# Hybrid attention and FFN pair on one core: the first row maxima of the plain layer from key differences, fills and masks on GpSimd, and the first causal maxima inside the last chunk turns

## The chip, the cores and the metric

The kernel runs on one core of a Trainium2 chip. The metric is the device time of one execution in microseconds; lower is better. The kernel before takes 1384.7 us (median of 3 runs, 1383.22 to 1387.49).

## The reference, cut to what matters

The input x has 4 sequences of 1024 tokens with 128 channels. Two layers follow each other, each an attention with 16 heads of 8 channels and then a gated FFN of width 384. The first attention is plain, the second causal. All of it is float32.

```python
x = x + attn_a(layernorm(x))      # softmax(q k / sqrt(8)) v, all keys
x = x + ffn(layernorm(x))         # silu(x wg) * (x wu), times wd
x = x + attn_b(layernorm(x))      # the same with keys after the query masked out
x = x + ffn(layernorm(x))
```

The softmax needs, for each head and query, the maximum of the scores over its keys. The change is about how and when the first of these maxima are taken.

## The kernel before, in words

**Windows.** Each layer has 16 windows: one sequence and a group of 4 heads. A window needs q and k of its heads as operands `qop` and `kop`. They are split in a high and a low part (`split_parts`, L746 for the subtraction, ScalarE's rounding copy L570), stored to DRAM and loaded again by SyncE (`store_parts` L343 and L345, `load_operands` L356 and L359, 14 transfers for a window) into one of 3 buffers. Rows of the operand buffers that no transfer fills hold ones (`kop`) or zeros (`qop`). For buffers 1 and 2 GpSimd sets the ones (L466) and ScalarE the zeros (`clear_query_rows`, L534).

**Jobs.** The row maxima come from "jobs". A job is one TensorE matmul (L993) of 128 queries with up to 512 keys into a bank of a ring in PSUM, and one VectorE reduction of that bank into a column of `maxima`: L804 (plain maximum), or L801 (add the causal mask, then maximum; a second instruction reads the accumulator) where the tile crosses the diagonal. In layer 0 a window has 64 jobs of 512 keys, two (kh 0 and 1) for each head and query block, in a ring of 4 banks (3 to 6). In layer 1 a window has 48 jobs of 128 to 512 keys and the ring has 3 banks (4 to 6).

**Shift.** When a half window (32 jobs in layer 0, 16 and 32 in layer 1) is done, VectorE negates and merges the maxima (`negate_max`, L810), GpSimd splits them in two bf16 parts (`split_shift`, L486, L488), TensorE transposes them (L1025), ScalarE copies them to `shift_rows` (L615), and SyncE moves them into rows of `qop` (`shift_to_operand`, two small transfers at L393). Only then can TensorE make the real scores of that half with the maximum subtracted (L1007, masks by L1015), ScalarE take the exponential (L599) and TensorE the weighted sums (L1041).

**Order.** All engines walk one list per layer, `plan.walk`, built from a string of letters: "job", "shift", "scores", "sums", "norm". Jobs run ahead of the scores: layer 0 starts with 48 jobs before its first scores (the shift of the first half stands behind job 37), layer 1 with 44 (its shift stands behind job 35). In these two heads of the walks the maxima run with little beside them. In layer 0 TensorE also transposes the FFN weights there (L969, after jobs 19, 23 and 27) and spreads the second layer's biases (L925 to L927), and GpSimd converts weights and builds the masks (L442 to L461) before the ones of L466. SyncE loads window 1's operands (`load_operands(1, 1)`) before it enters the walk, when both fills and all the stores of the last chunks are done. It works through its list in order, so a shift's transfers queue behind that load.

**Chunk turns.** Between the two attentions `stages` runs turns over 8 chunks of 512 tokens: output projection, residual, FFN, and, in layer 0, the qkv products of layer 1 for the chunk before. Turn 7 has `down(7)` (L1116), the addition to x (L726), the moments (L707, L711), `normalise` (L718) and the qkv products of chunk 6. Turn 8 has those of chunk 7 (L944, L946), with `add_v` (L737) and `split_parts`. Layer 1's walk begins after turn 8, though window 0's operands are loaded long before: by then all of sequence 0 is done.

## Time and profile before

| what | value |
|---|---|
| median of 3 runs | 1384.7 us |
| the profiled execution, its own time | 1387.37 us |
| its span, first to last instruction | 1385.3 us |
| mean granted TensorE clock | 0.967 |
| busy: TensorE, VectorE, ScalarE, GpSimd | 96%, 86%, 73%, 10% |

The sums of the prediction are made against the profiled execution, which is the longest of the runs shown. Busy shares are shares of the span; TensorE's records have modelled ends, so its share says little by itself. Times of instructions in the sections below are microseconds from the start of the span.

### The profile page before, as it was taken

The page shows a single profiled execution, that of the slowest core. Times are in us where ns is not written, and L with a number is a line of the kernel's source. Part 1 is how long each engine was busy: PE and PEld are TensorE (multiplying, and loading weights), DVE is VectorE, ACT ScalarE, POOL GpSimd, SP SyncE. Part 2 cuts the span into 40 slices and gives each one's busy share as a digit, 9 for nine tenths or more (in the row PEclk, how much of TensorE's full clock was granted, in tenths as well). Part 3 has the DMA queues.
Part 4 walks back from the last instruction along what each step waited for, and adds up shares of the span by engine and source line. Part 5 has one row for each costly group of instructions (what it writes and reads, how often), then busy time and mean ns, then how long its engine had stood idle before and what let it go on. Part 6 is the DMA issues. An engine that isn't in the chain of part 4 may idle for free.

```text
span 1385.3 us, 26773 instructions
## 1 busy us (share of the span) xinstructions
PE 1336.7 (96%) x9681; PEld 688.9 (50%) x9681; DVE 1193.6 (86%) x2979; ACT 1005.4 (73%) x1791; POOL 131.9 (10%) x301
## 2 busy tenths in 40 slices
PE   9899999999999999999997988999999999999898
PEld 6444444444444444444435765555555555555477
DVE  7899999999999999999935977788888888888366
ACT  8478888888888888888884542577777776777743
POOL 5320000000000000000001210200000000000011
PEclk9689999999999999999999995799999999999999
DMA  7611011111001111101000433122111211130001
GB/s 210 188 31 32 8 26 32 32 32 32 17 17 32 33 32 32 27 7 32 2 1 1 116 100 90 32 47 50 33 34 39 57 33 33 36 59 5 2 24 39
DMA packets 40059, 58.43 MB, mean 42 GB/s; under 512 B 7796, under 2 KB 19448, under 8 KB 39928
## 3 DMA queue, kind: packets, MB, share of 16 engines
q1 hardware_dynamic: 39928, 56.72, 17.2%
q8 instruction: 77, 1.26, 0.4%
q14 instruction: 54, 0.44, 0.1%
HBM read 36.77 MB, written 18.87 MB: 40 GB/s over the span
## 4 chain that ended last, share of the span: by engine, by line
PE 84%; DVE 7%; ACT 5%; issue 3%; DMA 0%; POOL 0%; DVEq 0%; SPq 0%; ACTq 0%; POOLq 0%
PE psum L1041 28%; PE psum L993 26%; PE psum L1007 16%; ACT probs L599 4%; PE psum L933 4%; PE psum L1116 3%; DVE maxima L804 3%; PE psum L1106 2%; PE psum L1015 2%; PE psum L944 1%; PE psum L1057 1%; DVE hid L870 1%; DVE junk L801 1%; PE psum L918 1%; PE psum L946 1%
## 5 line engine op out<-in xcount | busy, mean ns | idle before, releaser
L599 ACT ACTIVATE probs<-psum 128x512 f32<-128x512 f32 (+3 forms) x1408 | 833.7, 659 | 217.4 <-PE psum L1007 116.2
L804 DVE TENSOR_REDUCE maxima<-psum 128x1 f32<-128x512 f32 x1280 | 801.9, 681 | 29.5 <-PE psum L993 23.4
L993 PE MATMUL psum<-kop,qop 62*128 62x512 f32 (+3 forms) x1792 | 590.1, 448 | 11.0 <-DVE maxima L804 5.2
L1007 PE MATMUL psum<-qop,kop 64*128 64x512 f32 (+3 forms) x1792 | 526.0, 422 | 6.7 <-ACT probs L599 3.0
L993 PEld LDWEIGHTS psum<-kop,qop 62*128 62x128 f32 x1792 | 281.8, 192 | 394.3 <-DVE maxima L804 299.2
L1041 PE MATMUL psum<-probs,v 128*32 128x512 f32 (+3 forms) x3584 | 439.9, 563 | 0.7 <-ACT probs L599 0.7
L1007 PEld LDWEIGHTS psum<-qop,kop 64*128 64x128 f32 x1792 | 268.4, 188 | 76.1 <-ACT probs L599 44.6
L801 DVE CUSTOM_DVE_ANT_0 junk<-psum,mask 128x384 bf16<-128x384 f32 (+3 forms) x512 | 232.2, 485 | 53.5 <-PE psum L993 51.5
L1041 PEld LDWEIGHTS psum<-probs,v 128*32 128x32 f32 x3584 | 70.9, 108 | 100.9 <-issue 67.7
L1015 PE MATMUL psum<-half_ident,key_mask 64*128 64x64 bf16 x1024 | 89.6, 197 | 0.0
L496 POOL TENSOR_TENSOR att<-att_raw,rden 128x128 f32<-128x128 f32 x64 | 26.1, 407 | 512.4 <-DVE rden L815 512.4
L486 POOL TENSOR_TENSOR shift<-negmax,zeros 128x16 bf16<-128x16 f32 x64 | 14.1, 220 | 569.2 <-DVE negmax L810 569.2
L1106 PE MATMUL psum<-ffn_xt,gate_up_w 128*128 128x512 f32 x192 | 53.8, 417 | 5.4 <-DVE hid L870 5.3
L1015 PEld LDWEIGHTS psum<-half_ident,key_mask 64*128 64x128 bf16 x1024 | 49.5, 96 | 17.4 <-issue 7.3
L1116 PE MATMUL psum<-down_w,hid 128*128 128x128 f32 x384 | 46.4, 277 | 6.4 <-DVE hid L870 6.4
L678 ACT ACTIVATE hid<-psum 128x512 f32<-128x512 f32 x48 | 28.6, 597 | 30.7 <-PE psum L1106 30.4
L615 ACT CAST shift_rows<-psum 32x128 f32<-32x128 bf16 x64 | 16.0, 250 | 46.1 <-PE psum L1025 46.1
L1116 PEld LDWEIGHTS psum<-down_w,hid 128*128 128x128 f32 x384 | 44.1, 192 | 8.7 <-DVE hid L870 8.7
L815 DVE RECIPROCAL rden<-att_raw 128x16 f32<-128x16 f32 x64 | 15.6, 243 | 36.9 <-ACT att_raw L620 36.9
L726 DVE TENSOR_TENSOR x<-psum,x 128x512 f32<-128x512 f32 x32 | 22.1, 689 | 28.3 <-PE psum L1116 15.6
L933 PE MATMUL psum<-ident,sums 128*128 128x128 f32 x256 | 41.1, 283 | 5.0 <-ACT sums L606 1.6
L801 DVE DVE_READ_ACCUMULATOR2_ANT maxima<- 128x1 f32 x512 | 42.5, 83 | 0.1
(92 smaller groups left out, 693.7 us busy)
## 6 DMA issues: line engine op xcount, KB each, us to landing
qop<-q_parts SPq DMA_DIRECT2D x256, 64.0 KB
kop<-k_parts SPq DMA_DIRECT2D x64, 128.0 KB
kop<-k_parts SPq DMA_DIRECT2D x128, 64.0 KB
q_parts<-parts SPq DMA_DIRECT2D x24, 256.0 KB, 2.9
k_parts<-parts SPq DMA_DIRECT2D x24, 256.0 KB, 3.2
x<-in_L_attn_a_x SPq DMA_DIRECT2D x8, 256.0 KB, 4.8
q_parts<-att SPq DMA_DIRECT2D x8, 256.0 KB, 3.8
k_parts<-att SPq DMA_DIRECT2D x8, 256.0 KB, 3.7
```

Of the source, the lines that this page charges most:

```text
L496: nc.gpsimd.tensor_tensor(dst, att_raw[:, f, :, :, 0:HD], rden[:, f].rearrange("p t (h o) -> p t h o", o=1).broadcast_to([P, TPC, HG, HD]) ...
L599: nc.scalar.activation(probs[:, slot, heads[0] % 2:heads[-1] % 2 + 1, c0:], psum[:, bank:bank + len(heads), c0:], ACT.Exp, scale=SCORE_SCA ...
L678: nc.scalar.activation(hid[:, c, :], psum[:, 2 + 2 * (c % 2), :], ACT.Silu, scale=DEQUANT).then_inc(silu_ready, 1)
L801: nc.vector.tensor_tensor_reduce(out=junk[:, slot, 0:width], in0=src, in1=mask[:, CHUNK - width:], scale=1.0, scalar=LOWEST, op0=ALU.add, ...
L804: nc.vector.tensor_reduce(dst, src, AX_X, ALU.max).then_inc(ring_free, 1)
L933: ins = nc.tensor.transpose(psum[:, bank, t * P:(t + 1) * P], src[:, t, :], ident[:])
L993: mm(psum[:, bank, 0:width], qop[rows, buf, f, r, qb * P:(qb + 1) * P].bitcast(F32R), kop[rows, buf, r, kh * CHUNK:kh * CHUNK + width].bit ...
L1007: ins = mm(psum[:, bank + k, c0:], kop[rows, buf, c // 2, j * P:(j + 1) * P].bitcast(F32R), qop[rows, buf, f, c // 2, c0:].bitcast(F32R), ...
L1015: ins = mm(psum[:, bank + k, at:at + TILE_ROWS], key_mask[rows, part, :], half_ident[rows], start=False, stop=part == 1)
L1041: ins = mm(psum[32 * c:32 * c + 32, 7, c0:], v[:, at:at + 32], probs[:, slot, c % 2, c0:], start=(j == 0), stop=(s == plan.half_end[f]), t ...
L1106: ins = mm(psum[:, 2 + 2 * (c % 2) + k, :], gate_up_w[:, k, c, :].bitcast(F32R), ffn_xt[:, part].bitcast(F32R), start=part == 0, stop=part ...
L1116: ins = mm(psum[:, 7, t * P:(t + 1) * P], hid[:, c, t * P:(t + 1) * P], down_w[:, c, :], start=(c == 0), stop=(c == FB - 1))
```

## The change

**Pairs.** In layer 0 the first 48 jobs become 24 pairs. GpSimd makes `key_diff`, the first key half minus the second. TensorE makes the scores with the difference (a - b, banks 0 and 1) and with the second half (b, the job ring). ScalarE takes relu of the first into `excess` in SBUF, and one VectorE instruction (that of L801) adds the two and takes the maximum: max(a, b) = b + relu(a - b). Columns of `maxima` that a pair does not write hold the lowest number.

```diff
+            pool.wait_ge(operands_loaded[0], LOADS)
+            nc.gpsimd.tensor_tensor(key_diff[:].bitcast(F32R), kop[:, 0, :, 0:CHUNK], kop[:, 0, :, CHUNK:], ALU.subtract).then_inc(key_diff_ready, 1)
...
+            def two_pairs(plan, f, c, qb, pair):
+                if pair == 0:
+                    pe.wait_ge(key_diff_ready, 1)
+                if pair == SHIFT_PAIR:
+                    pe.wait_ge(probs_ready, 1)
+                for k in range(2):
+                    wait(pe, excess_ready, pair + k - 1)
+                    rows = slice(TILE_ROWS * k, TILE_ROWS * k + JOB_ROWS)
+                    mm(psum[:, (pair + k) % 2, :], qop[rows, 0, f, c // 2, qb * P:(qb + 1) * P].bitcast(F32R),
+                       key_diff[rows, c // 2, :].bitcast(F32R), start=True, stop=True).then_inc(diff_ready, 1)
+                for k in range(2):
+                    wait(pe, ring_free, 2 * (pair + k - 3))
+                    rows = slice(TILE_ROWS * k, TILE_ROWS * k + JOB_ROWS)
+                    mm(psum[:, plan.job_bank + (pair + k) % plan.job_ring, :], qop[rows, 0, f, c // 2, qb * P:(qb + 1) * P].bitcast(F32R),
+                       kop[rows, 0, c // 2, CHUNK:].bitcast(F32R), start=True, stop=True).then_inc(ring_full, 2)
...
+                def clip(pair):
+                    act.wait_ge(diff_ready, pair + 1)
+                    wait(act, ring_free, 2 * (pair - 3))
+                    nc.scalar.activation(excess[:, pair % 4], psum[:, pair % 2, :], ACT.Relu).then_inc(excess_ready, 1)
...
+            def run_pair(plan, f, c, qb, pair):
+                dve.wait_ge(ring_full, 2 * (pair + 1))
+                dve.wait_ge(excess_ready, pair + 1)
+                dve.sem_inc(begun, 1)
+                nc.vector.tensor_tensor_reduce(out=junk[:, pair % 4], in0=psum[:, plan.job_bank + pair % plan.job_ring, :],
+                                               in1=excess[:, pair % 4], scale=1.0, scalar=LOWEST, op0=ALU.add, op1=ALU.max,
+                                               accum_out=maxima[:, f, c, qb, 0:1]).then_inc(ring_free, 2)
```

The shift's transpose waits for 19 relus, pair 20 (`SHIFT_PAIR`) for the copy of the shift, the first scores for all 24 relus, and the first exponential for all 24 pairs. The weights are transposed into bank 2 at jobs 12, 20 and 28 and copied by ScalarE between the relus; the biases are spread at job 32.

**Fills and masks.** ScalarE's `clear_query_rows` for buffers 1 and 2 goes. GpSimd sets ones and zeros of buffer 1 (`fill_rows(1)`, four memsets of 32 x 2048) right behind the weights, ahead of the masks. Buffer 2 and the masks follow the first `split_shift`:

```diff
+            def fill_rows(buf):
+                for i in range(2):
+                    rows, done = slice(TILE_ROWS * i + GUARD_ROW, TILE_ROWS * i + SCORE_ROWS), 2 * (buf - 1) + i
+                    nc.gpsimd.memset(kop[rows, buf], 1.0).then_inc(key_rows, 1)
+                    pool.wait_ge(key_rows, done + 1)
+                    nc.gpsimd.memset(qop[rows, buf], 0.0).then_inc(query_rows, 1)
+                    pool.wait_ge(query_rows, done + 1)
...
                     if kind == "shift":
                         split_shift(w, f)
+                        if layer == 0 and (w, f) == (0, 0):
+                            pool.wait_ge(shift_ready, 1)
+                            fill_rows(2)
+                            make_masks()
+                            pool.wait_ge(masks_ready, 6)
```

**Early causal maxima.** TensorE makes jobs 0 to 17 of layer 1, and VectorE takes jobs 0 to 21, inside turns 7 and 8. TensorE makes jobs 0 to 2 before `down(7)` and 3 to 8 between its tiles, 9 to 11 behind it, 12 to 14 ahead of the transpose of chunk 7's rows and 15 to 17 ahead of its qkv products. The q and k products of chunks 6 and 7 go to banks 2 and 3 in place of 4 and 5.

```diff
+                    last_qkv = layer == 0 and m >= CHUNKS - 1
+                    if last_qkv:
+                        causal_jobs(*((0, 9) if m == CHUNKS - 1 else (15, 18)))
                     if residual is not None:
                         g = layer * CHUNKS + residual
                         dve.wait_ge(down_psum, g + 1)
...
                     if qkv_rows is not None:
                         if qkv_rows == 0:
                             dve.wait_ge(sums_done, WINDOWS * PLANS[0].n)
+                        if qkv_rows == CHUNKS - 2:
+                            causal_jobs(9, 12)
                         add_v(1, qkv_rows, qkv_rows % 2, 1)
...
                     if qkv_rows is not None:
+                        if last_qkv:
+                            causal_jobs(*((12, 15) if m == CHUNKS - 1 else (18, 22)))
                         split_parts(1, qkv_rows, qkv_rows % 2)
```

The rest of both walks is as before.

## Rows read from the trace of the kernel before

**Rows 1.** The page, part 1: busy time and share of each engine.
```profile
PE 1336.7 (96%) x9681; PEld 688.9 (50%) x9681; DVE 1193.6 (86%) x2979; ACT 1005.4 (73%) x1791; POOL 131.9 (10%) x301
```
**Rows 2.** Windows: us, busy of PE, PEld, DVE, ACT, POOL, then PEclk, DMA share, GB/s.
```profile
38.00:84.00 46.00, 41.67 (x135) 22.28 (x134) 42.32 (x74) 20.57 (x29) 13.10 (x18) 0.63 0.40 125
84.00:700.00 616.00, 611.74 (x3985) 258.54 (x3977) 598.67 (x1017) 518.44 (x1048) 33.62 (x91) 1.00 0.12 26
826.00:884.00 58.00, 50.00 (x205) 28.39 (x206) 41.79 (x148) 19.21 (x25) 11.42 (x9) 0.59 0.30 73
```
**Rows 3.** Timeline, head of layer 0: start us, length us, VectorE and TensorE.
```profile
41.44 1.22 DVE L746 TENSOR_TENSOR att<-qk,att 128x1024 f32<-128x1024 f32 x1 [1.74 <-ACT att L570]
42.59 19.49 DVE L804 TENSOR_REDUCE maxima<-psum 128x1 f32<-128x512 f32 x32
...
71.75 0.62 PE L1007 MATMUL psum<-qop,kop 64*128 64x512 f32 x1
```
**Rows 4.** Groups by form, 884 to 1320 us: busy us, mean ns, idle before.
```profile
L804 DVE TENSOR_REDUCE maxima<-psum 128x1 f32<-128x512 f32 x236 | 152.2, 681 | 8.8 <-PE psum L993 8.8
...
L801 DVE CUSTOM_DVE_ANT_0 junk<-psum,mask 128x512 bf16<-128x512 f32 x116 | 75.3, 685 | 1.2 <-issue 0.4
```
**Rows 5.** Timeline, ScalarE: the zero fills, and a run of exponentials.
```profile
41.44 7.23 ACT L534 CAST qop<-zeros 32x4096 fp32r<-32x4096 f32 x2
...
80.22 4.28 ACT L599 ACTIVATE probs<-psum 128x512 f32<-128x512 f32 x8 [0.57 <-PE psum L1007]
```
**Rows 6.** The chain that ended last, 36 to 90 us: start us, us, what.
```profile
53.08 0.83 PE psum L969 x3
...
71.95 0.43 PE psum L1007
...
85.23 0.23 PE psum L1007
```
**Rows 7.** Timeline, GpSimd and SyncE's queue, head of layer 0.
```profile
45.77 0.51 POOL L446 MEMSET mask<- 128x512 f32 x1
...
49.69 7.07 POOL L466 MEMSET kop<- 32x4096 f32 x2
...
56.92 1.72 SPq L356 DMA_DIRECT2D qop<-q_parts  x4
...
62.24 1.14 SPq L359 DMA_DIRECT2D kop<-k_parts  x3
...
84.42 9.00 POOL L515 TENSOR_TENSOR x<-x,bvo 128x4096 f32<-128x4096 f32 x1
```
**Rows 8.** Timeline, VectorE: the last chunk turns and job 22 of layer 1.
```profile
826.23 0.69 DVE L726 TENSOR_TENSOR x<-psum,x 128x512 f32<-128x512 f32 x1 [3.04 <-PE psum L1116]
...
837.02 0.88 DVE L737 TENSOR_TENSOR v<-psum,bvo 128x128 f32<-128x128 f32 x4 [4.94 <-PE psum L946]
837.91 1.22 DVE L746 TENSOR_TENSOR parts<-qk,parts 128x1024 f32<-128x1024 f32 x1
...
850.06 0.28 DVE L801 CUSTOM_DVE_ANT_0 junk<-psum,mask 128x128 bf16<-128x128 f32 x1
```
**Rows 9.** Timeline, SyncE's queue and TensorE: start of layer 1's first scores.
```profile
843.24 1.71 SPq L356 DMA_DIRECT2D qop<-q_parts  x4
...
857.34 12.30 SPq L393 DMA_DIRECT2D qop<-shift_rows  x4
...
860.80 1.12 PE L1007 MATMUL psum<-qop,kop 64*128 64x512 f32 x2
```
**Rows 10.** Timeline, ScalarE: copies of the shift, layer 1, windows 0 to 2.
```profile
868.09 0.26 ACT L615 CAST shift_rows<-psum 32x128 f32<-32x128 bf16 x1 [2.69 <-PE psum L1025]
891.84 0.26 ACT L615 CAST shift_rows<-psum 32x128 f32<-32x128 bf16 x1 [0.25 <-PE psum L1025]
901.38 0.25 ACT L615 CAST shift_rows<-psum 32x128 f32<-32x128 bf16 x1 [1.17 <-PE psum L1025]
919.86 0.26 ACT L615 CAST shift_rows<-psum 32x128 f32<-32x128 bf16 x1 [0.25 <-PE psum L1025]
```

More of the change, by code:

```diff
@@ L64, in __init__ @@
         self.job_bank = 7 - job_ring
+        self.paired = range(0 if causal else jobs_ahead)
         self.steps = []
@@ L133 @@
               jobs_ahead=44, sums_behind=1, project_at=(4, 6, 10))]
+SHIFT_PAIR = 20
+assert [item[0] for item in PLANS[0].walk].index("shift") in range(2 * SHIFT_PAIR - 3, 2 * SHIFT_PAIR + 1)
+PE_JOBS_AHEAD, DVE_JOBS_AHEAD = 18, 22
+assert all(item[0] == "job" for item in PLANS[1].walk[:DVE_JOBS_AHEAD])
 def transformer_pair_kernel(nc, x_in, wqkv_a, bqkv_a, wout_a, bout_a, wqkv_b, bqkv_b, wout_b, bout_b,
@@ L469, in inverse_deviation @@
+            pool.wait_ge(masks_ready, 1)
+            fill_rows(1)
             def inverse_deviation(k, mo, count):
```

205 lines of the change are left out of this document (125 added, 80 removed).

## The prediction, made before the change was run

> **What bounds the kernel now.** I read the page first, then windows by stage, then timelines of the stages that the change touches. TensorE's records cover 96% of the span, VectorE's 86% [rows 1]. The windows show where that mean misleads [rows 2]: from 84 to 700 us both engines are nearly always busy (612 and 599 of 616 us) at full clock, and no part of the change lies there. The two heads of the walks are different: from 38 to 84 us and from 826 to 884 us the granted clock is 0.63 and 0.59, and ScalarE is busy for 21 of 46 and 19 of 58 us. A microsecond saved there moves everything behind it forward, because the walks behind are unchanged.
>
> In the head of layer 0, VectorE ends its last split at 42.66 us and then does jobs at 19.49 / 32 = 0.61 us each [rows 3]. TensorE starts the first scores at 71.75 us. That is about 48 x 0.61 = 29.3 us: VectorE sets the pace, TensorE waits for banks and ScalarE mostly idles. In the head of layer 1, VectorE starts its jobs behind the split that ends at 839.13 us, takes 22 of them until 850.06 us [rows 8], and the first scores start at 860.80 us [rows 9]. Ahead of it, in turns 7 and 8, VectorE waited 3.04 and 4.94 us for TensorE [rows 8].
>
> **Part 1, pairs.** VectorE loses 48 reductions and gets 24 instructions of L801's kind. At 512 keys that lasts 685 ns against 681 ns for the plain reduction [rows 4], so I take the same pace, 0.61 us: 24 x 0.61 = 14.6 us. ScalarE's relu is not in the trace. The nearest row is the exponential from PSUM at the same size, 4.28 / 8 = 0.54 us each [rows 5]; bounds are a half of that and the 0.61 us at which it would tie with VectorE; I take 0.54 us. It hides beside VectorE. TensorE still makes 48 matmuls, two for each pair: one takes 0.23 us at full clock and 0.43 us at half clock [rows 6], so a pair costs it 0.46 or 0.86 us. At half clock TensorE therefore becomes the bound. The weight transposes (three groups of 0.83 us) and the bias spread, which I count as a fourth such group, then come on top [rows 6].
> - All at full clock: 42.66 + 14.6 = 57.3 us, plus a stall at the shift. Relu 19 stands behind the shift's copy in ScalarE's order, which needs VectorE's L810 after pair 16, GpSimd, TensorE and ScalarE. I estimate some 2 us of chain, of which two pairs (1.2 us) hide a part: 1 us is left. 58.3 us.
> - All at half clock: 42.66 + 24 x 0.86 + 4 x 0.83 = 66.6 us, plus 0.5 us of stall: about 67 us.
> - Mixed, which I take: the clock falls as before, because TensorE has the same gap ahead, but at half clock TensorE now works without a gap, as it did from 71.75 us on, some 6 us before its matmul was back at 0.23 us [rows 3, 6]. That is 7 pairs and one transpose group at half clock (6.0 + 0.8 us); the other 17 pairs take 10.4 us at VectorE's pace, with the other groups beside them. 42.66 + 6.8 + 10.4 + 1 = 60.9 us.
>
> **The queue in front of the shift.** This decides. Scores need the shift's transfers, and SyncE issues them behind window 1's load. That load began at 56.92 us, right behind L466's end at 56.76 us, and its last issue ended at 63.38 us: 6.46 us [rows 7]. Before, this was over when the shift came. Now GpSimd leaves the masks out ahead of the fills (it started them at 45.77 us) and makes four memsets of 2048 columns. Two of 4096 took 7.07 us, so four of half that are again about 7.1 us [rows 7]. With the bf16 identity (0.3 us) and four short waits they end at 45.77 + 0.3 + 7.1 + 0.4 = 53.6 us; SyncE issues the load until 60.1 us, and only then the shift. In layer 1 the first scores came 860.80 - 857.34 = 3.46 us after that issue began [rows 9]. That is an upper bound for the transfer; the lower one is about 2 us. First scores: 60.1 + 3.5 = 63.6 us, say 63.7 us, behind the 60.9 us of the pairs. **Part 1 gives 71.75 - 63.7 = 8.0 us** (4.5 if all is at half clock, 9.5 if the transfer is quick).
>
> `key_diff` is a quarter of L515's columns: 9.00 / 4 = 2.25 us [rows 7]. It can start when window 0's operands have landed, before TensorE could use them, and ScalarE is not free for the first relu before 41.44 us, where it began its fills [rows 5]. I cost it at nothing; if the operands land as late as 39.7 us, it and the first relu put VectorE back by about 0.4 us. The 7.23 us of fills that leave ScalarE [rows 5] lay beside VectorE's jobs: nothing. Buffer 2 and the masks on GpSimd end some 11 us after the first shift, by about 66 us, ahead of the second one: nothing. The extra memset of `maxima` at the start: nothing.
>
> **Two rules weighed.** By rows, relu on ScalarE costs 0.54 us in a lane that idles, and on VectorE it would cost 0.61 us in the lane that bounds [rows 4, 5]. The Trainium skill, ScalarE: Activation LUTs, Rules for kernel authors, says to use VectorE, not ScalarE, for relu and max; by that rule 24 more VectorE instructions would come on top (24 x 0.61 = 14.6 us) and eat the gain, and the trace disagrees with it for this float32 operand in PSUM. The split L746 reads two tensors from SBUF and lasts 1.22 us [rows 3], and `key_diff` reads two on GpSimd. The Trainium skill, SBUF — State Buffer, Who interferes with whom, says that such a pair takes turns on one port; by it one of them could be late by up to the other's length, 1.22 us (an estimate), and no row shows it.
>
> **Part 2, early causal jobs.** VectorE does 22 jobs in turns 7 and 8: 850.06 - 839.13 = 10.9 us of work [rows 8]. The waits that can take them are 3.04 + 4.94 = 8.0 us and some short ones [rows 8], so at least 2 us must come out as delay. By order I get more. TensorE's jobs 3 to 8 stand between the tiles of `down(7)`: +0.9 us before x. Jobs 9 to 11 stand ahead of `add_v(6)` and `normalise(7)`, where GpSimd's part had hidden add_v: +1 us. Job 17 needs the bank of job 14, which VectorE takes after `normalise(7)`, and chunk 7's products stand behind job 17 on TensorE: +0.7 us. Jobs 18 to 21 stand ahead of `split_parts(7)`: +1.6 us, less what a TensorE kept busier gives back of its clock, about 0.8 us. The split ends at 839.13 + 3.4 = 842.5 us, and job 22 starts there in place of 850.06 us: 7.5 us ahead. Again the queue cuts it. Behind the split come the stores, and window 1's load began 843.24 - 839.13 = 4.1 us later [rows 8, 9]. It takes some 5.8 us of issuing; it now runs from 846.6 to 852.4 us. TensorE comes to the shift about 7.5 us earlier, at 849 us, and SyncE holds it until 852.4 us. First scores at 852.4 + 3.46 = 855.9 us in place of 860.80 us: **part 2 gives 4.9 us** (4 to 7).
>
> **Sum.** 1387.4 - 8.0 - 4.9 = 1374.5 us against the profiled execution. That one is 2.7 us above the median, so 1371.8; I say **1372.0 us**.
>
> **The rivals.**
> 1. *Half clock through all pairs.* TensorE bounds the pairs, scores start at 67 us, part 1 gives 4.5 us. For it: before, no job ahead of the scores brought the clock back. Against it: TensorE then had gaps. 1375.5 us. Chance 0.15.
> 2. *The clock comes back earlier in layer 1.* From the second shift of window 0 to the first of window 1 it took 23.75 us, and 18.48 us one window later [rows 10]: the half clock cost 5.3 us there. If the earlier start meets the full clock, most of that is saved: about 1367.5 us. Chance 0.13.
> 3. *The early jobs give nothing.* The delays in turns 7 and 8 with a half clock on chunk 7's products grow to 7 us or more, and only part 1 is left: 1376.5 to 1379 us. That includes the change that does not do what it says, relus or waits costing more than VectorE saves. Chance 0.09.
> 4. *Slower: half clock for the windows behind.* In layer 1's first windows TensorE bounds. Half clock costs 5.27 us in 18.48 us of work, 0.22 us per us of cold time (5.27 / 23.75) [rows 10]. If matmuls thinned out over turns 7 and 8 and the held shift leave the clock low, it needs 12.9 / 0.22 = 58 us more of it to eat the gain and some 78 us to come to +4.2 us: 1389 us. For it: the clock is already low over much of 826 to 884 us. Against: from 84 to 700 us it was never low [rows 2]. Chance 0.03.
>
> **How the numbers follow.** The forecast has 0.60. Its own range is 1369 to 1375.5 us. Rivals 1 and 2 lie close on both sides; with the spread of single runs (some 2 us to each side of the median) the range is 1365.5 to 1379.5 us, and leaves out rival 4, most of rival 3's far end and a part of rival 2. About 0.3% (4.2 us) is what a measurement of this kernel can tell from no change. Faster than 1380.5 us: 0.90, all but rival 4 and a part of rival 3; the same 0.07; slower 0.03.
>
> **What the profile after would show.** Right: 24 VectorE instructions behind 42.7 us at about 0.61 us each for most of them, relus of 0.54 us beside them, GpSimd's four memsets ended near 53.6 us, SyncE's load up to 60 us with the shift directly behind it, first scores near 63.7 us; job 22 near 842.5 us and first scores of layer 1 near 856 us. Wrong: VectorE waiting for TensorE at 0.86 us a pair (rival 1); first scores directly behind the pairs, with no wait for the shift (then the queue was not the bound); a split of chunk 7 that ends beyond 846 us (rival 3); a granted clock of 0.5 beyond 884 us less the gain (rival 4).

## The result, and the profile after

The changed kernel takes 1373.09 us (median of 4 runs, 1371.79 to 1376.02), the kernel before 1385.19 us beside it (median of 4, 1383.22 to 1387.49). The ratio is 0.991, with a 95% interval of 0.9895 to 0.9925: 12.1 us faster. The same kernel was run again later, on another occasion (`e12_after_again` below): 1376.61 us, ratio 0.9937 (0.9925 to 0.9949). So the two measurements put the gain at 0.9% and 0.6% (12.1 and 8.2 us in the medians), with intervals that together reach from 0.5% to 1.05%. The forecast of 1372.0 us (range 1365.5 to 1379.5, "faster" 0.90) holds in both.

The profiled execution took 1372.5 us (span 1370.7 us, mean granted clock 0.974), 14.9 us less than that of before. The page, part 1, against [rows 1]:

```profile
PE 1322.5 (96%) x9681; PEld 678.7 (50%) x9681; DVE 1180.1 (86%) x2979; ACT 1010.7 (74%) x1813; POOL 141.6 (10%) x309
```

No share moved by more than a point. The instruction counts of VectorE agree (2979), because 24 pairs make 24 instructions and 24 reads of an accumulator where 48 reductions stood. The gain can't be seen here, only in the two stretches.

**Layer 0.** The timeline of VectorE, against [rows 3] (start us, length us; in brackets the idle time before it and what ended it):

```profile
40.66 1.22 DVE L790 TENSOR_TENSOR att<-qk,att 128x1024 f32<-128x1024 f32 x1 [1.93 <-ACT att L602]
41.80 0.68 DVE L839 CUSTOM_DVE_ANT_0 junk<-psum,probs 128x512 bf16<-128x512 f32 x1
...
47.90 0.69 DVE L839 CUSTOM_DVE_ANT_0 junk<-psum,probs 128x512 bf16<-128x512 f32 x1 [1.13 <-ACT probs L697]
...
51.85 0.69 DVE L839 CUSTOM_DVE_ANT_0 junk<-psum,probs 128x512 bf16<-128x512 f32 x1 [1.16 <-ACT probs L697]
...
58.94 0.69 DVE L839 CUSTOM_DVE_ANT_0 junk<-psum,probs 128x512 bf16<-128x512 f32 x1 [1.74 <-ACT probs L697]
...
60.39 0.69 DVE L839 CUSTOM_DVE_ANT_0 junk<-psum,probs 128x512 bf16<-128x512 f32 x1 [0.75 <-issue]
```

The groups of 41.5 to 67 us on VectorE (busy us, mean ns; idle before, by releaser):

```profile
L839 DVE CUSTOM_DVE_ANT_0 junk<-psum,probs 128x512 bf16<-128x512 f32 x24 | 15.5, 687 | 6.7 <-ACT probs L697 6.0 <-issue 0.8
```

The instruction itself is as cheap as its model in [rows 4] (687 against 685 ns). But the 24 of them hold 6.7 us of idle time, nearly all of it waiting for ScalarE's relu. Each stall of 1.1 to 1.7 us follows the weight transposes or the biases; the 0.75 us at 60.39 stand behind the shift's transpose and copy (forecast 1 us). TensorE, same timeline:

```profile
39.87 0.50 PE L1054 MATMUL psum<-key_diff,qop 62*128 62x512 f32 x2 [2.06 <-POOL key_diff L459]
...
43.84 1.28 PE L1054 MATMUL psum<-key_diff,qop 62*128 62x512 f32 x2
44.43 1.11 PE L1059 MATMUL psum<-kop,qop 62*128 62x512 f32 x2
45.47 0.90 PE L1042 MATMUL psum<-ident,probs 128*128 128x128 f32 x3
46.30 0.79 PE L1054 MATMUL psum<-key_diff,qop 62*128 62x512 f32 x2
46.90 0.63 PE L1059 MATMUL psum<-kop,qop 62*128 62x512 f32 x2
...
63.62 0.79 PE L1077 MATMUL psum<-kop,qop 62*128 62x512 f32 x1 [0.65 <-DVE maxima L839]
64.21 0.63 PE L1107 MATMUL psum<-qop,kop 64*128 64x512 f32 x1
```

ScalarE, same timeline:

```profile
43.19 1.08 ACT L697 ACTIVATE probs<-psum 128x512 f32<-128x512 f32 x2 [0.39 <-PE psum L1054]
44.66 1.09 ACT L697 ACTIVATE probs<-psum 128x512 f32<-128x512 f32 x2 [0.39 <-PE psum L1054]
47.13 1.08 ACT L697 ACTIVATE probs<-psum 128x512 f32<-128x512 f32 x2 [1.38 <-PE psum L1054]
```

First scores: 64.21 us, against 71.75 us. Not all of these 7.54 us are the change's. VectorE's last split starts at 40.66 us here and at 41.44 us before [rows 3], and such a difference comes from run to run of one program: the last qkv products start on TensorE at 36.75 us here and at 38.15 us in the second profile of the same kernel (`e12_after_again`). From the last split to the first scores it was 71.75 - 41.44 = 30.31 us and is 64.21 - 40.66 = 23.55 us: 6.8 us less.

The rhythm is a loop between two engines, over two difference banks. TensorE fills a bank only when its relu has freed it. For one bank, taken singly from the trace: a relu runs from 43.19 to 43.78 us, the bank's next matmul from 43.84 to 44.63, the next relu starts at 44.66 us. So a bank turns in 44.66 - 43.19 = 1.47 us, 0.60 of it relu and 0.79 from the start of the matmul to its end, and with two banks that is 0.74 us for a pair. It is this round trip that sets the pace, and not TensorE's work: where both banks are free, behind the transposes, the two difference matmuls and the two behind them start 46.90 - 46.30 = 0.60 us apart, which would be 0.60 us a pair. At a transpose group the loop grows from 1.47 to 47.13 - 44.66 = 2.47 us, and VectorE has nothing to cover it with.

GpSimd's fills, same timeline, against [rows 7]:

```profile
45.34 1.80 POOL L472 MEMSET kop<- 32x2048 f32 x1
...
50.90 1.80 POOL L474 MEMSET qop<- 32x2048 f32 x1
```

SyncE's queue, same timeline:

```profile
52.80 1.72 SPq L370 DMA_DIRECT2D qop<-q_parts  x4
...
57.87 2.07 SPq L373 DMA_DIRECT2D kop<-k_parts  x3
59.99 1.41 SPq L407 DMA_DIRECT2D qop<-shift_rows  x2
```

The fills end at 52.70 us (forecast 53.6), the load at 59.94 (60.1), and the shift is issued at 59.99. The shift's copy on ScalarE had ended at 59.73, so the queue was not what the scores waited for: their matmul stands behind a job that waited 0.65 us for VectorE.

**Layer 1.** VectorE, against [rows 8]:

```profile
806.38 0.69 DVE L770 TENSOR_TENSOR x<-psum,x 128x512 f32<-128x512 f32 x1 [2.44 <-PE psum L1228]
...
818.95 0.69 DVE L770 TENSOR_TENSOR x<-psum,x 128x512 f32<-128x512 f32 x1 [0.47 <-PE psum L1228]
...
831.20 0.88 DVE L781 TENSOR_TENSOR v<-psum,bvo 128x128 f32<-128x128 f32 x4 [2.06 <-PE psum L1018]
...
833.62 1.22 DVE L790 TENSOR_TENSOR parts<-qk,parts 128x1024 f32<-128x1024 f32 x1
834.75 0.28 DVE L856 CUSTOM_DVE_ANT_0 junk<-psum,mask 128x128 bf16<-128x128 f32 x1
...
849.63 1.29 DVE L859 TENSOR_REDUCE maxima<-psum 128x1 f32<-128x512 f32 x2 [2.87 <-PE psum L1077]
```

The waits of 3.04 and 4.94 us in turns 7 and 8 are now 0.47 and 2.06 us. To compare the two traces here, a common mark is needed that lies ahead of the early jobs: turn 6's addition to x. In the kernel before it is

```profile
815.13 0.69 DVE L726 TENSOR_TENSOR x<-psum,x 128x512 f32<-128x512 f32 x1 [2.44 <-PE psum L1116]
```

Timeline of the kernel after, SyncE's queue, against [rows 9]:

```profile
838.50 1.71 SPq L370 DMA_DIRECT2D qop<-q_parts  x4
...
843.17 1.14 SPq L373 DMA_DIRECT2D kop<-k_parts  x3
844.36 12.18 SPq L407 DMA_DIRECT2D qop<-shift_rows  x4
```

TensorE, the first scores of layer 1, against [rows 9]:

```profile
848.08 0.79 PE L1107 MATMUL psum<-qop,kop 64*128 64x512 f32 x2 [2.29 <-DMA qop<-shift_rows]
```

ScalarE, copies of the shift, against [rows 10]:

```profile
841.36 0.25 ACT L646 CAST shift_rows<-psum 32x128 f32<-32x128 bf16 x1 [9.63 <-PE psum L1125]
...
855.00 0.26 ACT L646 CAST shift_rows<-psum 32x128 f32<-32x128 bf16 x1 [2.69 <-PE psum L1125]
877.01 0.25 ACT L646 CAST shift_rows<-psum 32x128 f32<-32x128 bf16 x1 [0.25 <-PE psum L1125]
```

The shift's rows are ready at 841.61 us, and SyncE issues them at 844.36 us, behind window 1's load: held for 2.75 us (forecast 3.4, from 849 to 852.4 us). TensorE waits 2.29 us for them.

**Where the 14.9 us lie.** Before minus after, at marks that both traces have:

| mark | before | after | ahead by | added here |
|---|---|---|---|---|
| first scores, layer 0 | 71.75 | 64.21 | 7.54 | 7.54 |
| turn 6's addition to x | 815.13 | 806.38 | 8.75 | 1.21 |
| first scores, layer 1 | 860.80 | 848.08 | 12.72 | 3.97 |
| second shift of window 0 | 868.09 | 855.00 | 13.09 | 0.37 |
| first shift of window 1 | 891.84 | 877.01 | 14.83 | 1.74 |
| first shift of window 2 | 919.86 | 904.84 | 15.02 | 0.19 |

Of the first 7.54 us, 0.8 are the earlier start. A part of the later ones is the clock. Windows of the kernel before (the columns are those of [rows 2]):

```profile
730.00:750.00 20.00, 15.29 (x97) 10.85 (x98) 8.09 (x28) 8.83 (x16) 1.68 (x3) 0.91 0.00 1
...
850.00:884.00 34.00, 31.94 (x152) 18.05 (x153) 24.58 (x85) 13.79 (x18) 9.72 (x5) 0.50 0.19 38
```

The same windows of the kernel after, and the pairs':

```profile
40.00:66.00 26.00, 23.34 (x74) 12.59 (x74) 18.17 (x53) 16.31 (x34) 19.09 (x19) 0.54 0.57 176
...
730.00:750.00 20.00, 15.35 (x109) 13.73 (x109) 15.49 (x54) 9.13 (x15) 4.10 (x7) 1.00 0.00 1
...
850.00:884.00 34.00, 33.40 (x275) 17.94 (x269) 25.51 (x86) 20.89 (x30) 10.13 (x6) 0.78 0.14 33
```

Around 740 us the change touches nothing (the same work lies 8 to 9 us earlier in the kernel after). Before had a short stretch at half clock there and after had none, and the 1.21 us of the second mark go with that: between the first two marks the four profiles without such a stretch (this one, `e3_fills_only`, `e6_busy_order` and `e7_order` below) take 742.2 to 742.6 us, and the kernel before 743.4 us. From 850 to 884 us the clock was 0.50 before and 0.78 after: it came back inside window 0, which gave the 1.74 us of the fifth mark.

### The profile page after: what moved, and what is told of

Same layout as the page of the kernel before. It is cut to its first block, busy times and chain, and to the rows that moved or that the text cites. A ratio compares the mean times of both kernels' runs of the same rounds, so it can differ in the third digit from the quotient of the medians.

```text
span 1370.7 us, 26878 instructions
## 1 busy us (share of the span) xinstructions
PE 1322.5 (96%) x9681; PEld 678.7 (50%) x9681; DVE 1180.1 (86%) x2979; ACT 1010.7 (74%) x1813; POOL 141.6 (10%) x309
## 4 chain that ended last, share of the span: by engine, by line
PE 83%; DVE 7%; ACT 5%; issue 3%; SPq 1%; DMA 1%; POOL 0%; DVEq 0%; ACTq 0%; POOLq 0%
PE psum L1141 28%; PE psum L1077 24%; PE psum L1107 16%; ACT probs L630 4%; PE psum L1005 3%; PE psum L1228 3%; DVE maxima L859 3%; PE psum L1212 2%; PE psum L1115 2%; PE psum L1016 1%; DVE hid L935 1%; PE psum L1157 1%; PE psum L1054 1%; DVE junk L856 1%; PE psum L990 1%
## 5 line engine op out<-in xcount | busy, mean ns | idle before, releaser
L859 DVE TENSOR_REDUCE maxima<-psum 128x1 f32<-128x512 f32 x1232 | 773.6, 682 | 31.5 <-PE psum L1077 25.8
L1077 PE MATMUL psum<-kop,qop 62*128 62x512 f32 (+3 forms) x1744 | 561.6, 437 | 7.0 <-DVE maxima L856 1.5
L1077 PEld LDWEIGHTS psum<-kop,qop 62*128 62x128 f32 x1744 | 267.0, 188 | 376.9 <-DVE maxima L859 285.2
L597 ACT ACTIVATE qk<-psum,bqk 128x512 f32<-128x512 f32 x32 | 21.1, 682 | 31.5 <-PE psum L1016 31.4
```

The costliest lines, as they stand in the source:

```text
L859: nc.vector.tensor_reduce(dst, src, AX_X, ALU.max).then_inc(ring_free, 1)
L1077: mm(psum[:, bank, 0:width], qop[rows, buf, f, r, qb * P:(qb + 1) * P].bitcast(F32R), kop[rows, buf, r, kh * CHUNK:kh * CHUNK + width].bit ...
```

## The experiments

All of them start from the changed kernel. Each was compared with the kernel before, run beside it; that one took 1387.5 us (median) beside the first four, 1384.5 us beside the next four and 1384.8 us beside the last four.

### The parts alone

`e1_no_early` keeps pairs and fills and takes the early jobs away.

```diff
-PE_JOBS_AHEAD, DVE_JOBS_AHEAD = 18, 22
+PE_JOBS_AHEAD, DVE_JOBS_AHEAD = 0, 0
...
             def causal_jobs(first, last):
-                jobs_and_negations(1, PLANS[1].walk[first:last])
+                pass
...
```

TensorE's `causal_jobs` becomes `pass` in the same way.

> The changed kernel without the early causal jobs: pairs and fills stay, all 44 first jobs of layer 1 run behind turn 8 again. Theory (the parts add): the pairs bring the first scores of layer 0 forward by 7 us (7.54 in the profiles, 0.8 of it a start that differed), and that stays to the end: 1378 us, with first scores of layer 1 about 53.4 us of span behind those of turn 7's addition to x as before (45.7 us). Rival 1 (the gain is mostly the clock's luck around the chunk turns and layer 1's head): 1382 us or more. Rival 2 (early jobs only move what the queue takes back): 1374 us.

`e2_no_pairs` keeps early jobs and fills. The first 48 jobs are plain again, without `key_diff` and relus.

```diff
-        self.paired = range(0 if causal else jobs_ahead)
+        self.paired = range(0)
...
```

> The changed kernel without the pairs: 48 single jobs and their 48 plain maxima again in layer 0, no key difference, no relu; fills, masks and early causal jobs stay. Theory (the parts add): first scores of layer 0 stay near 71.5 us, the early jobs give about 4 us up to the first scores of layer 1, and up to 2 us more if the clock rises earlier there: 1379 to 1381 us. Rival (the early jobs only pay in company of the pairs): 1384 us or more.

`e3_fills_only` makes both edits, so what is left is the fills and masks on GpSimd.

> Neither pairs nor early jobs; only the fills and masks on GpSimd in their new order, bank 2 for the weights, banks 2 and 3 for the last products. Theory: the fills of ScalarE were hidden behind VectorE's jobs, so 1385 us, within 0.15% of the kernel before, first scores of layer 0 at 71 to 72 us. Rival (the fills held the first shift or the load in front of something): 1380 to 1383 us.

| kernel | median us | ratio (95%) | first scores, layer 0 | x of turn 6 | first scores, layer 1 | behind x |
|---|---|---|---|---|---|---|
| before | 1387.50 | 1 | 71.75 | 815.13 | 860.80 | 45.67 |
| fills only | 1386.37 | 0.9994 (0.998 to 1.0008) | 71.28 | 813.90 | 859.55 | 45.65 |
| pairs and fills | 1380.15 | 0.9944 (0.993 to 0.9958) | 65.82 | 810.02 | 856.37 | 46.35 |
| early jobs and fills | 1381.95 | 0.9957 (0.9941 to 0.9973) | 71.70 | 817.34 | 859.06 | 41.72 |

(The marks of before are those of its trace above. The ratios come from all runs and differ a little from those of the medians.) The fills alone give nothing that can be measured. Against them, the pairs give 0.9994 - 0.9944 = 0.50% (6.9 us) and the early jobs 0.9994 - 0.9957 = 0.37% (5.1 us); by the medians it is 6.2 and 4.4 us. By the intervals, each of these differences is known to some 0.2% (3 us). Within that the parts add up to the whole, neither needs the other, and the third rival (early jobs give nothing) falls. The times lie 1 to 2 us above what was expected. From the last split to the first scores the pairs save 30.37 - 23.84 = 6.5 us here (40.91 to 71.28 us and 41.98 to 65.82 us), as the 6.8 us above.

The column "behind x" leaves the clock ahead of turn 6 out. The early jobs bring layer 1's first scores 4.0 us nearer in both kernels that have them (41.72 and 41.70 against 45.67 us). That these two agree so well is chance: in `e12_after_again`, the same program, it is 40.05 us, and in `e7_order`, with the same layer 1, 43.53 us, so 2.1 to 5.6 us nearer. In the trace of `e2_no_pairs` the same wait stands on TensorE, longer still:

```profile
859.06 0.79 PE L1102 MATMUL psum<-qop,kop 64*128 64x512 f32 x2 [4.14 <-DMA qop<-shift_rows]
```

### The queue ahead of the shift

Theory: in layer 1 the shift's wait behind window 1's load costs up to 2.3 us of TensorE's time. `e4_act_shift` has ScalarE issue the two transfers right behind its own copy, in its own queue.

```diff
-                        shift_to_operand(f, w % BUFS, unit_base + number)
+                        if not (layer == 1 and (w, f) == (0, 0)):
+                            shift_to_operand(f, w % BUFS, unit_base + number)
...
                         nc.scalar.copy(shift_rows[:, f, :], psum[0:rows, bank, 0:P // 2].bitcast(BF16)).then_inc(probs_ready, 1)
+                        if layer == 1 and (w, f) == (0, 0):
+                            act.wait_ge(probs_ready, unit_base + number + 1)
+                            for i in range(2):
+                                row, half = TILE_ROWS * i + SHIFT_ROW, SHIFT_PARTS * PAIRS * TPC
+                                nc.scalar.dma_start(qop[row:row + SHIFT_PARTS, w % BUFS, f],
+                                                    shift_rows[half * i:half * (i + 1), f, :]).then_inc(shift_loaded[f], SEM_DMA)
```

> The changed kernel, but the two transfers of layer 1's first shift are issued from ScalarE's queue, right behind its copy, and no longer stand behind window 1's load in SyncE's queue. Theory (SyncE's queue holds the shift by 844.36 - 841.61 = 2.75 us, and TensorE waited 2.29 us for it): TensorE's wait for the shift vanishes, first scores of layer 1 come 2.3 us earlier, 1370.8 us. Rival (the half clock on TensorE sets the pace behind, or window 1's operands are late next): within 0.5 us of the changed kernel.

Measured: 1373.3 us, ratio 0.99 (0.9883 to 0.9916), not apart from the change's 0.991. Its timeline, ScalarE's queue:

```profile
847.98 1.90 ACTq L652 DMA_DIRECT2D qop<-shift_rows  x2
```

and TensorE:

```profile
853.23 0.79 PE L1114 MATMUL psum<-qop,kop 64*128 64x512 f32 x2 [1.10 <-DMA qop<-shift_rows]
```

From issue to scores it takes 853.23 - 847.98 = 5.25 us, against 848.08 - 844.36 = 3.72 us behind the load. From the copy's start to the scores it is 5.5 us against 6.7 us, so of the 2.75 us in the queue only 1.2 us show as gain. TensorE's wait of 1.10 us is no fair measure: chunk 7's products met a half clock here, and the copy itself came 37.5 us behind turn 6's x, where it was 35.0 us.

It is tempting to say that the transfer is slower because it runs beside the load from another queue. Other profiles don't bear that out. With the shift behind the load on SyncE's own queue, the same stretch took 3.74 us in `e12_after_again`, but 5.41 us in `e2_no_pairs`, 5.08 in `e5_busy`, 5.35 in `e6_busy_order` and 5.59 in `e7_order`; each time TensorE stood waiting for the shift. What makes it 3.7 us in some profiles and over 5 us in others is open. A gain of 1.2 us is below what these runs resolve.

`e7_order` asks the same of layer 0: the shift is issued ahead of window 1's load.

```diff
-                load_operands(1, 1)
+                if layer == 1:
+                    load_operands(1, 1)
...
                             shift_to_operand(f, w % BUFS, unit_base + number)
+                        if layer == 0 and (w, f) == (0, 0):
+                            load_operands(1, 1)
```

> The changed kernel with only the order changed: in layer 0 SyncE issues the first shift ahead of window 1's load. Theory (at half clock VectorE's last pair ends as late as the shift arrives): first scores at 63.6 to 64.2 us, 1373 us, no gain. Rival (the queue alone bounds the first scores, as predicted): 2.5 us earlier, 1370.5 us.

Measured: 1373.35 us, 0.9927 (0.9912 to 0.9943). The shift is issued at 59.75 us and the first scores start at 64.14 us, against 59.99 and 64.21 us. With the load out of its way nothing moved: in layer 0 the pairs decide, and the load merely ended at the same moment.

### The clock of TensorE

The granted clock is 0.5, the lower of its two levels (1.2 GHz of 2.4), from about 42 to 72 us, and again from about 834 us, with a short stretch at 827 to 831 us ahead of it. Theory: what the engine leaves idle ahead of and between the pairs holds it there; matmuls of the identity, whose results nobody reads, should keep it up. `e5_busy` puts 15 ahead of the first pair, 4 behind it and 2 behind each later two pairs.

```diff
+            def fill_gap(bank, count):
+                for _ in range(count):
+                    mm(psum[:, bank, 0:P], ident[:], ident[:], start=True, stop=True)
...
                 if layer == 0:
+                    fill_gap(0, 10)
                     pe.wait_ge(qk_ready, 2 * CHUNKS)
                     pe.wait_ge(v_ready, CHUNKS)
+                    fill_gap(7, 5)
...
+                if pair < 16:
+                    fill_gap(7, 4 if pair == 0 else 2)
```

> The changed kernel with matmuls of the identity added on TensorE: 15 before the first pair, 4 behind it and 2 behind each later two pairs up to pair 15. They write to a bank that nobody reads; nothing else changes. Theory (the half clock slows the pairs, and behind them SyncE's queue holds the shift): the granted clock stays at 1.0 from 40 us to about 52 us, VectorE takes pairs at 0.61 us for most of them and its waits in this stage fall from 6.7 to below 3.5 us, but the shift still comes out behind window 1's load at about 60 us, so first scores stay at 63.5 to 64.2 us and the time within 1 us of the changed kernel (1373). Rival (the pairs alone bound the first scores): first scores at 60.5 us or before, 1370 us.

`e6_busy_order` is `e5_busy` and `e7_order` together.

> The added matmuls of the last kernel, and in layer 0 SyncE issues the first shift ahead of window 1's load. Theory (both the pairs and the queue bound the first scores together): first scores at 60 to 61 us, 3 us earlier than in the changed kernel, 1370 us. Rival (only one of them bounds): no better than the other two kernels of this call that change one of them.

`e9_busy_both` adds such matmuls in layer 1's head to `e6_busy_order`: 6 ahead of chunk 7's transpose, 2 behind each job of 512 keys up to job 43, 1 behind a shorter one, and 6 more behind job 43.

```diff
                     if kind == "job":
                         run_job(layer, w, what, number)
+                        if layer == 1 and number < 44:
+                            fill_gap(7, 2 if what[4] == CHUNK else 1)
+                        if layer == 1 and number == 43:
+                            fill_gap(7, 6)
...
                     if qkv_rows == CHUNKS - 1:
                         causal_jobs(12, 15)
+                        fill_gap(7, 6)
```

> As the second kernel of this call, with identity matmuls on TensorE also in layer 1's head: 6 ahead of the transpose of chunk 7, 2 behind each job of 512 keys and 1 behind each shorter one up to job 43, 6 more before the first scores. Theory (the half clock from 826 to 868 us costs several microseconds behind the first scores): the granted clock stays at 1.0 over 826 to 880 us in the profile and the time falls by another 3 to 5 us, to about 1366 us, with a smaller spread of runs. Rival (VectorE and the shift set this head anyway, and the dummies delay the jobs): within 1 us of the second kernel of this call, or slower.

Windows of `e9_busy_both` (columns as in [rows 2]):

```profile
40.00:54.00 14.00, 14.00 (x89) 9.96 (x88) 10.51 (x30) 10.09 (x19) 10.59 (x10) 1.00 0.77 269
54.00:66.00 12.00, 10.26 (x46) 6.45 (x45) 9.55 (x26) 8.43 (x19) 8.68 (x10) 0.75 0.21 55
...
826.00:850.00 24.00, 23.93 (x106) 15.54 (x106) 17.45 (x48) 3.96 (x5) 0.43 (x2) 1.00 0.44 112
850.00:884.00 34.00, 33.36 (x301) 18.49 (x304) 27.11 (x91) 20.66 (x30) 10.15 (x6) 1.00 0.14 34
```

The clock does as it is told: full until about 60 us, and full all through layer 1's head. In layer 0 the first scores come earlier, and the time does not; in layer 1 it pays, at a price.

- Layer 0, `e5_busy`: 1377.31 us, 0.9953 (0.9937 to 0.9968), expected 1373. First scores at 63.08 us, 1.1 us ahead of the change's. Since the starts differ, count from the last qkv products on TensorE (36.75 us in the change, 37.65 here): 25.4 us in place of 27.5. VectorE's waits are 5.1 us in place of 6.7, where below 3.5 was expected; 1.60 of them stand ahead of the first pair. The 15 matmuls there last 3.62 us by the trace, where TensorE's gap was 2.06 us, so a part of what the clock gives is spent before it. At full clock a transpose group still stalls VectorE, by 0.63 us in place of 1.16.
- `e6_busy_order`: 1376.21 us, 0.9943 (0.9931 to 0.9955), first scores at 62.50 us (expected 60 to 61), 25.0 us behind the products, here too behind a job that waited for VectorE.
- The medians of both are above that of `e7_order` beside them, by 4.0 and 2.9 us, though their first scores come 2 us earlier. Their profiles show no stretch that costs it, and these two lie low among their runs. The mean clocks of all runs point elsewhere in the program: 20 us less at half clock in this head should add about 0.0075 to the mean, and the medians of the means are 0.977 in both and 0.9745 in `e7_order`. So the typical run lost clock at other places. Why is open.
- Both layers, `e9_busy_both`: 1371.67 us, 0.9908 (0.9895 to 0.9921), 1370.42 to 1371.88 in 4 runs, the narrowest spread of all. It was expected 3 to 5 us below `e6_busy_order`, from which it differs by layer 1's matmuls alone, and is 4.5 us below it, with intervals that don't meet. Against `e7_order`, without any added matmul, it is 1.7 us, and the intervals meet.

Layer 1 is the instructive half. Distances behind turn 6's addition to x:

| kernel | first scores, layer 1 | first shift of window 1 |
|---|---|---|
| before | 45.67 | 76.71 |
| after | 41.70 | 70.63 |
| `e9_busy_both` | 48.24 | 71.41 |

The added matmuls stand in the way of the jobs, and the first scores come 6.5 us later than in the change. Yet by the next window all but 0.8 us of that is made good: from the first scores to window 1's shift it takes 877.68 - 854.51 = 23.17 us, where the change takes 877.01 - 848.08 = 28.93 us. Of these 5.8 us, 3.7 lie behind the second shift of window 0 (877.68 - 859.32 = 18.36 us against 877.01 - 855.00 = 22.01), and they are the clock's: one window later, at full clock in both, the like stretch takes 18.3 us in both. The other 2.1 us lie ahead of it, where VectorE's maxima, given more time by the late start, may have helped as well; that was not separated. So half clock costs 3.7 to 5.8 us behind the first scores, about as much as was won by starting them earlier; but whoever buys the clock with matmuls in front gives most of it back in front.

`e13_busy_l1` tries it cheaper, in layer 1 alone: 4 ahead of the transpose, one behind each job of 512 keys, 3 ahead of the scores.

> The changed kernel with identity matmuls on TensorE in layer 1's head only: 4 ahead of the transpose of chunk 7, one behind each job of 512 keys up to job 43, 3 more before the first scores. In the earlier kernel with two dummies a job VectorE waited about 10 us for TensorE in this head, and still the time was the best; one dummy fits into VectorE's 0.61 us a job. Theory (the half clock behind the first scores of layer 1 costs 3.5 to 5.3 us): the clock stays at 1.0 from 826 us on, first scores come within 1 us of the changed kernel's (41.7 us behind turn 6's addition to x), the copy of window 1's first shift follows that of window 0's second by 18.5 us in place of 22.0, and the time is 3 to 4 us below the changed kernel of this call. Rival (what is gained in clock is lost to the dummies again): within 1 us of it.

Measured: 1377.81 us, 0.9956 (0.9943 to 0.9968), beside the unchanged change's 0.9937. The theory that few will do fell. The clock went to half at about 835 us all the same, and there each added matmul costs more. TensorE, `e13_busy_l1`:

```profile
834.70 0.49 PE L1047 MATMUL psum<-ident 128*128 128x128 f32 x2
836.41 0.79 PE L1047 MATMUL psum<-ident 128*128 128x128 f32 x2
```

The first scores start at 852.80 us, 45.6 us behind x: the early jobs' gain is gone. From the second shift of window 0 to the first of window 1 it takes 22.06 us, where 18.5 was expected.

`e10_tuned` takes the thin form everywhere, 6 ahead of the first pair and one behind each two pairs, with `e7_order`'s order and `e13_busy_l1`'s head; `e11_tuned_act` adds ScalarE's issue of layer 1's shift as in `e4_act_shift`.

> As the last kernel, and in layer 0's head 6 identity matmuls ahead of the first pair, one behind each two pairs up to pair 15 (15 and 2 before, which held the first pair back by 1.6 us), and the first shift ahead of window 1's load. Theory: pairs at full clock at 0.65 us on average, first scores at 60.5 to 61 us, 3 us before the changed kernel's; together with layer 1's head 6 us below it: 1367 us. Rival (in layer 0's head the clock is worth nothing, since the first scores' half clock costs no VectorE time): as the last kernel.

> As the last kernel, with the first shift of layer 1 issued from ScalarE's queue. Theory (with the clock kept up TensorE reaches the first scores earlier and stands longer at the shift that SyncE holds): another 1 to 1.5 us below. Rival (the transfer itself is slow beside window 1's load, as it was before: 5.1 us from issue to the first scores): less than 0.7 us.

Measured: 1374.32 us, 0.9923 (0.991 to 0.9936), and 1374.27 us, 0.993 (0.9914 to 0.9945). The 1367 us expected of the first is missed. In layer 0 this is the best form: full clock until about 55 and 58 us, first scores at 61.54 and 60.72 us, which is 23.5 and 23.0 us behind the last qkv products, where the change has 27.5. So the head's half clock costs 4 us up to the first scores. ScalarE's issue gives nothing more, and could not: with the added matmuls TensorE no longer waits for the shift in either kernel.

`e12_after_again` is the changed kernel, unchanged, beside them.

> The changed kernel itself, unchanged, as the reference of this call: 0.9905 to 0.992 of the kernel before on this chip, runs spread over 4 to 6 us, because the moments at which the clock falls and rises differ from run to run.

Measured: 1376.61 us, 0.9937 (0.9925 to 0.9949), outside the 0.9905 to 0.992 expected. Its profiled execution (1377.77 us) is 5.3 us longer than that of the result, and the marks say where:

| mark | result's profile | `e12_after_again` | behind by |
|---|---|---|---|
| first scores, layer 0 | 64.21 | 66.62 | 2.41 |
| turn 6's addition to x | 806.38 | 811.62 | 5.24 |
| first scores, layer 1 | 848.08 | 851.67 | 3.59 |
| first shift of window 1 | 877.01 | 882.34 | 5.33 |

Windows of `e12_after_again`:

```profile
730.00:750.00 20.00, 14.59 (x80) 12.56 (x76) 10.90 (x41) 7.82 (x13) 3.98 (x7) 0.83 0.00 1
826.00:850.00 24.00, 18.39 (x59) 10.19 (x57) 23.16 (x75) 6.76 (x9) 1.69 (x4) 0.80 0.48 131
850.00:884.00 34.00, 31.89 (x216) 16.52 (x216) 21.14 (x75) 18.98 (x25) 10.14 (x6) 0.64 0.14 33
```

Most of the 2.41 us at the first mark are not the clock's. 1.4 us are there already when the last qkv products start (38.15 against 36.75 us), and another 0.6 us come before the first difference matmul. There a second thing differs. GpSimd's `key_diff`, which reads two tensors from SBUF, runs from 37.52 to 39.87 us, and VectorE's split ahead of the last, which reads two as well, starts just behind it:

```profile
37.68 3.26 DVE L790 TENSOR_TENSOR att<-qk,att 128x1024 f32<-128x1024 f32 x1 [0.17 <-ACT att L602]
```

It lasts 3.26 us in place of 1.22 and ends 1.1 us behind `key_diff`: it stood still while the other ran. In `e7_order` the split comes first (36.38 us, 1.22 us long), and `key_diff`, started at 36.52 us, lasts 3.29 us in place of 2.35. In the result's profile they hardly meet (the split from 36.29 to 37.52 us, `key_diff` from 37.28 us).

Behind that the clock has its part. The same program meets its half clock at other times: here at 738 to 745 us too (0.83 against 1.00), and up to the second mark another 2.83 us are lost; and in window 0 until about 874 us, where the stretch between the shifts again takes 882.34 - 858.59 = 23.75 us, as before the change. The two profiles of one program differ by 5.3 us, a third of the 14.9 us between the profiles of before and after. No kernel here is clearly faster than the change: `e9_busy_both` has the lowest median and the same ratio as the first result, and `e10_tuned` is 2.3 us below `e12_after_again` beside it with overlapping intervals.

## Why the prediction was right

Forecast 1372.0, measured 1373.09 and 1376.61 us. The mechanism, the two heads of the walks, was right, and the sum of 12.9 us is near what the parts alone give (6.9 + 5.1 us, by the medians 6.2 + 4.4, and nothing for the fills). Inside it several terms were off and partly made up for each other. That part 1's term came out near is luck in its steps.

- **VectorE's price.** 24 x 0.61 us: right, 687 ns for the instruction and 0.61 us from one start to the next where nothing is awaited.
- **The mixed clock.** This step failed. It said that a TensorE without gaps would be back at full clock some 6 us into the pairs. Its records from 42 us on are nearly without gaps, and the clock stayed at 0.5 until about 72 us. The first rival's premise, half clock through all pairs, was the true one. `e10_tuned` and `e11_tuned_act`, at full clock for most of the pairs, price it at 4 us of the first scores.
- **A pair at half clock.** This too was mis-sized, the other way. I took 2 x 0.43 = 0.86 us and TensorE as the bound. TensorE needs no more than 0.60 us for the two; what bounds is the round trip of relu and matmul over two banks, 1.47 us for two pairs, 0.74 us for one. At full clock it is 45.53 - 44.34 = 1.19 us from relu to relu (`e10_tuned`), less than two of VectorE's 0.61 us. The text counted no such loop.
- **The transposes.** I put them beside VectorE's work at full clock and added them at half clock. The trace shows a stall of 1.13 to 1.16 us for each of three groups and 1.74 us at the biases, so 5.2 of the 6.7 us of idle time are these four; with two banks for the differences nothing is in stock when TensorE does something else (no run tried a third). At full clock they don't vanish either: 0.63 us each in `e5_busy`.
- **The end of the pairs.** Together: 22.4 us from the first pair's start at 41.80 us to the end of the last at 64.17 us, where the mixed clock gave 18.2 us and all at half clock 24.4 us.
- **The queue.** Fills ended 0.9 us and the load 0.2 us earlier than forecast, but it didn't decide: `e7_order` took it away and won nothing. The first scores at 64.21 us (forecast 63.7) came from the pairs. That the two ended together is a coincidence, and a forecast right to 0.5 us for the wrong reason; behind the last split, where the start that differed is left out, part 1 gave 6.8 us and not 8.0. I should have noticed that a pair chain and a queue a few us apart are both candidates, with a price for each; the text had them at 60.9 and 63.7 us.
- **`key_diff`.** 2.44 us (forecast 2.25), and it ended at 39.72 us, the late case that the text named. TensorE waited 2.06 us for it, but VectorE's first pair started right behind its split, so it cost nothing there. In other runs it did meet a split, and one of the two stood still: 2.04 us for VectorE's in `e12_after_again`, 0.9 us for `key_diff` in `e7_order`. This is the second of the two rules weighed in the prediction; its estimate of up to 1.22 us was too small, since `key_diff` is the longer one.
- **Relu.** 1.08 us for two on ScalarE, the 0.54 us of [rows 5]. By the Trainium skill, ScalarE: Activation LUTs, Rules for kernel authors, it would stand on VectorE. There 24 x 0.61 = 14.6 us would have met 6.7 us of idle time, so at least 7.9 us of it would be added by this estimate, more than part 1 gives. No run tried it. But ScalarE's relu was not free of the path either: it makes 0.60 of the 1.47 us of a bank's round trip.
- **Early jobs.** Job 22 starts 834.75 - 806.38 = 28.37 us behind turn 6's x, where before it was 850.06 - 815.13 = 34.93: 6.56 us earlier, forecast 7.5. The split's delay is the term: it ends 28.46 us behind x against 24.00 us, so 4.5 us and not 3.4. A half clock on chunk 7's products (827 to 831 us) is in that: in `e12_after_again`, without it, the split ends 838.40 - 811.62 = 26.78 us behind x, 2.8 us late. The store and the load took as long as expected (838.50 - 834.84 = 3.66 us, then 5.81 us of issuing), and shift to scores 3.72 us for 3.46 (over 5 us in four other profiles). Sum: 3.97 us, forecast 4.9 and its lower bound 4; between profiles it goes from 2.1 to 5.6 us.
- **The rivals.** The second (clock back earlier in layer 1) came in part in the first profile, 1.74 us of the 5.3 us, and not at all in `e12_after_again`. The third fell by `e2_no_pairs`. Of the fourth nothing was seen: from 884 to 1280 us the clock is full in both profiles.

Weighed by the marks, then: 6.8 us forecast as 8.0, 4.0 us forecast as 4.9, together 10.8 of the 12.9 us, and some 4 us between the two profiles that no term of the sum named: 0.8 us of earlier start, the clock, and small shifts of the walk behind. In the medians it is 12.1 and 8.2 us against 12.7. The first measurement lies nearer to the forecast than the terms do, and that is luck of starts and clock.

## What to carry to other kernels

Halving the work of the engine that bounds a stretch exposes the loop behind it: count the buffers between the engines (two banks here), take the round trip of one buffer through both engines, divide it by their number, and ask, for every foreign piece of work on TensorE or ScalarE, whether they hold enough in stock to cover it. Price a start-up stretch at both clock levels and take marks in the trace, well ahead of the change, as the origin; the start that differed and the clock's comings and goings elsewhere were some 4 us of a difference of 15. Profile one program twice before reading 2 us out of two profiles. Where two chains end within a few us, take one away by experiment before calling the other the bound.

## What the hardware showed that I had not expected

- Records with hardly a gap did not bring the clock back. From 40 to 66 us TensorE's records cover 23.34 of 26 us at a clock of 0.54, and it came back only about 72 us, where the scores had begun. With the added matmuls in `e9_busy_both` (14.00 of 14.00 us) it never fell until about 60 us.
- Where it falls and rises differs between runs of one program: at 740 us in some (0.91 before, 0.83 in `e12_after_again`) and not in others (1.00 after); back in window 0 at about 868 or about 874 us.
- Two matmuls of 62 rows and 512 columns started together at half clock, and the next two 0.60 us behind them, less than twice 0.43 us. The two of a pair of jobs use different rows of the array, and their records overlap; that this is the reason was only argued.
- The two small transfers of a shift took at most 3.46 to 3.74 us from issue to use in some profiles and 5.08 to 5.59 us in others, behind a load on the same queue or beside it on another. What decides is open.
- A split on VectorE and `key_diff` on GpSimd, each with two operands in SBUF, don't run together: the later of them stood still for 2.04 us (`e12_after_again`) or about 0.9 us (`e7_order`).
